# A graph attention layer on one core: the first two row groups summed in two halves of the neighbours

## The chip, the cores and the metric

The kernel runs on one core of one Trainium2 chip. The metric is device time in microseconds of one execution; lower is better. A core has TensorE (PE), VectorE (DVE), ScalarE (ACT), GpSimd (POOL), SyncE (SP) and 16 DMA engines.

## What is computed

```python
h = jnp.maximum(_layernorm(x, axis=-1), 0.0)
H = h @ W_fc + b_fc
scores = (H @ w_att[:d])[:, None] + (H @ w_att[d:])[None, :] + b_att
scores = jnp.where(adj > 0, scores, NEG_INF)
alpha = jax.nn.softmax(scores, axis=1)
out = x + alpha @ H
```

x is 4096 x 128 float32, adj is 4096 x 4096 int32 (67.1 MB). A row's own term and b_att are the same for all its neighbours and leave the softmax unchanged; neighbour j has the weight w_j = exp(H_j . w_att[d:] - bound), and a row's result is the sum of w_j * H_j over its neighbours, divided by the sum of their w_j. A row without neighbours gets the mean of H.

## The kernel before

The neighbours j are 32 tiles of 128. For each, `features[:, t]` holds w_j * (h_j @ W) and w_j, each as a part with few bits (high) and the rest (low): 258 columns. The rows i of the result are 32 tiles too, in five groups (`GROUPS`: 6, 7, 8, 7, 4 row tiles). A row tile's sum takes one PSUM bank (`BANKS`). For each group the kernel runs over all 32 tiles of neighbours: the adjacency, transposed on the host, is loaded into `ring`, VectorE turns the integers into a 0/1 `mask`, and PE multiplies the mask's 128 x 128 blocks with the features, one matmul (a "sum") of 258 columns per block, 1024 in all.

A unit (`UNITS`) is two tiles of neighbours of one group (four for the last group); two units are a pair, and a pair is one load: 72 units, 36 pairs. `ring` has 4 slots of a pair, `mask` 4 places of a unit. SP issues the load of a pair when the units that had its slot are masked (`slot_free`, line 282; load at line 304). VectorE masks a unit when it has landed and when PE has finished the unit four before it (`mask_free`, line 270; `mask_unit`, instruction at line 497). From unit 20 on ScalarE makes the last 512 columns of most masks (`share`, line 442).

Features are made from x in the first 70 us, four tiles (a chunk) at a time: VectorE's statistics (line 512) and `deviations`, ScalarE's ReLU (line 383), PE's transposes against `ident` (`turn`, line 837), ScalarE's copy (`take_turned`, line 362), PE's product with W (`features_of`, line 848), ScalarE's weighting (`weigh`, line 372), VectorE's `split` (lines 590 and 593) and ScalarE's `take_high` (line 378). Splits 0 to 2 are tiles 0 to 3, split u from 3 on is chunk u - 2, so splits 6 to 9 are tiles 16 to 31. GpSimd builds `ident` with an affine_select (line 343) and then spreads the attention vectors (`a_wide`, line 347), from which PE makes `v_rows` (line 822, copied at 393).

Each engine runs its own program in order, written out by hand: VectorE's masks, splits and other work in lines 636 to 775, PE's in lines 913 to 941. A waiting instruction holds up all behind it on its engine. When a group ends, ScalarE copies its banks to `sums` (line 455), and VectorE divides them and adds them to x (`inverse_of`, `add_sums`, `add_means`) between the masks of later groups. The row sums for the mean (line 704) stand behind masks 18 to 25. The first and last pairs of units of a group go row tile by row tile (`by_rows`, it wants both masks of the pair), so that banks come free one by one; the others go tile by tile (`by_tiles`).

## Time and profile before

| | us |
|---|---|
| median of 3 runs | 210.57 |
| lowest, highest | 207.68, 211.06 |
| the profiled execution | 207.97 |
| its span, first to last instruction | 206.2 |
| busy: PE, VectorE, ScalarE, GpSimd | 152.5, 144.5, 69.0, 1.7 |

The DMA engines moved 71.67 MB at a mean of 348 GB/s. Times in a trace count from the start of the span. A share of busy time is an average over parts with different limits, so the rows below are read by stretch.

### The profile page before, as it was taken

The numbers are of one execution on the slowest core, as the hardware profiler recorded it, in microseconds if no ns is written. First come the engines' busy times: TensorE is split into PE (matmuls) and PEld (weight loads), VectorE is DVE, ScalarE is ACT, GpSimd is POOL, SyncE is SP. The second block draws the span as 40 slices with busy tenths as digits, with TensorE's granted clock in tenths as the row PEclk, the third lists the DMA queues.
The fourth block names the chain that finished last, engine by engine and source line by source line (L and its number), as shares of the span: only waits on it lengthen the run. The fifth ranks groups of instructions, "written<-read, shape, count | busy, mean of one in ns | idle before, by whom it ended". The sixth has DMA issues, their size and how long they took to land.

```text
span 206.2 us, 3218 instructions
## 1 busy us (share of the span) xinstructions
PE 152.5 (74%) x1130; PEld 144.1 (70%) x1130; DVE 144.5 (70%) x446; ACT 69.0 (33%) x157; POOL 1.7 (1%) x10
## 2 busy tenths in 40 slices
PE   0058973946695599999767988875999997689940
PEld 0026962846694599989766988765999986688930
DVE  2415999992643969999644557788689967358992
ACT  2206655670662145432430222222522234502100
POOL 1010000000000000000000000000000000000000
PEclk9999999696999999999999999998799999999995
DMA  6999991715286699999999999999999999999821
GB/s 175 397 420 437 378 415 43 246 65 191 114 317 198 248 409 415 428 445 421 432 424 429 420 429 426 429 421 428 434 417 434 424 413 442 429 415 399 344 99 54
DMA packets 7940, 71.67 MB, mean 348 GB/s; under 512 B 881, under 2 KB 1650, under 8 KB 3314
## 3 DMA queue, kind: packets, MB, share of 16 engines
q1 hardware_dynamic: 7344, 71.18, 84.2%
q10 hardware_dynamic: 578, 0.26, 0.5%
q8 instruction: 10, 0.16, 0.3%
q14 instruction: 8, 0.07, 0.1%
HBM read 69.34 MB, written 2.10 MB: 346 GB/s over the span
## 4 chain that ended last, share of the span: by engine, by line
DMA 43%; DVE 23%; PE 16%; issue 10%; ACT 4%; POOL 0%; DVEq 0%; POOLq 0%; ACTq 0%
DMA ring<-adj 43%; PE bank L867 11%; DVE mask L497 9%; DVE features L518 2%; DVE x_sb L618 2%; ACT weighted L372 2%; PE bank L848 2%; DVE stats L512 2%; DVE weighted L704 1%; ACT relu_T L362 1%; PE bank L837 1%; DVE high_bits L590 1%; PE bank L827 1%; DVE features L593 1%; ACT relu L383 1%
## 5 line engine op out<-in xcount | busy, mean ns | idle before, releaser
L867 PE MATMUL bank<-features,mask 128*128 128x258 f32 x1024 | 135.9, 292 | 26.4 <-DVE mask L497 22.9
L867 PEld LDWEIGHTS bank<-features,mask 128*128 128x128 f32 x1024 | 129.8, 196 | 31.8 <-DVE mask L497 27.2
L497 DVE TENSOR_SCALAR mask<-ring 128x1536 fp32r<-128x1536 int32 (+3 forms) x70 | 65.9, 957 | 29.6 <-DMA ring<-adj 24.8
L442 ACT ACTIVATE mask<-ring,half_steep 128x512 fp32r<-128x512 int32 x39 | 26.1, 716 | 68.4 <-DMA ring<-adj 68.4
L618 DVE SCALAR_TENSOR_TENSOR x_sb<-sums,inv_den,x_sb 128x128 f32<-128x128 f32 x56 | 17.3, 347 | 0.6
L455 ACT COPY sums<-bank 128x258 f32<-128x258 f32 x28 | 10.5, 374 | 14.1 <-PE bank L867 12.1
L848 PE MATMUL bank<-w_sb,relu_T 128*128 128x128 f32 x64 | 10.0, 303 | 6.3 <-ACT relu_T L362 6.3
L848 PEld LDWEIGHTS bank<-w_sb,relu_T 128*128 128x128 f32 x64 | 8.7, 211 | 7.6 <-ACT relu_T L362 7.6
L372 ACT ACTIVATE weighted<-bank,w_over_std 128x128 f32<-128x128 f32 x32 | 9.2, 368 | 9.2 <-PE bank L848 7.5
L383 ACT ACTIVATE relu<-x_sb,neg_mean 128x128 f32<-128x128 f32 x32 | 9.8, 390 | 4.9 <-DVE neg_mean L527 4.9
L822 PE MATMUL bank<-w_T_and_a,a_wide 128*128 128x128 f32 x2 | 0.8, 488 | 12.9 <-POOL a_wide L347 12.9
L512 DVE BATCH_NORM_STATS2 stats<-x_sb 128x6 f32<-128x128 f32 x32 | 6.7, 279 | 4.1 <-DMA x_sb<-x 4.0
L822 PEld LDWEIGHTS bank<-w_T_and_a,a_wide 128*128 128x128 f32 x2 | 0.5, 313 | 12.8 <-issue 12.8
L590 DVE TENSOR_SCALAR high_bits<-weighted 128x512 int32<-128x512 int32 (+2 forms) x10 | 3.7, 371 | 7.8 <-ACT weighted L372 7.7
L631 DVE SCALAR_TENSOR_TENSOR x_sb<-mean_H,is_empty,x_sb 128x128 f32<-128x128 f32 x32 | 9.1, 347 | 0.0
L518 DVE SCALAR_TENSOR_TENSOR features<-relu,v_rows 128x128 fp32r<-128x128 f32 x32 | 8.6, 285 | 0.0
L704 DVE SCALAR_TENSOR_TENSOR weighted<-relu,rstd,weighted 128x128 f32<-128x128 f32 x28 | 7.9, 345 | 0.0
L362 ACT COPY relu_T<-bank 128x512 f32<-128x512 f32 x8 | 4.7, 592 | 8.3 <-PE bank L837 8.3
L378 ACT CAST features<-high_bits 128x512 fp32r<-128x512 f32 (+2 forms) x10 | 5.4, 537 | 3.3 <-DVE high_bits L590 3.2
L593 DVE TENSOR_TENSOR features<-weighted,high_bits 128x512 fp32r<-128x512 f32 (+2 forms) x10 | 5.9, 586 | 0.3
L837 PE MATMUL bank<-ident,relu 128*128 128x128 f32 x32 | 6.0, 321 | 0.1
L837 PEld LDWEIGHTS bank<-ident,relu 128*128 128x128 f32 x32 | 4.6, 168 | 1.3 <-issue 1.1
(72 smaller groups left out, 46.3 us busy)
## 6 DMA issues: line engine op xcount, KB each, us to landing
ring<-adj SPq DMA_DIRECT2D x16, 1792.0 KB, 13.4
ring<-adj SPq DMA_DIRECT2D x11, 2048.0 KB, 17.1
ring<-adj SPq DMA_DIRECT2D x7, 1536.0 KB, 8.0
ring<-adj SPq DMA_DIRECT2D x2, 768.0 KB, 6.9
x_sb<-x SPq DMA_DIRECT2D x1, 1024.0 KB, 13.6
ring<-adj SPq DMA_DIRECT2D x1, 1024.0 KB, 15.6
ring<-adj SPq DMA_DIRECT2D x4, 256.0 KB, 15.9
out<-x_sb SPq DMA_DIRECT2D x2, 448.0 KB, 10.0
```

What stands on the lines that cost most here:

```text
L372: last = nc.scalar.activation(weighted[:, u % 2, at], ps_features[:, of], ACT.Copy, scale=w_over_std[:, t:t + 1])
L383: nc.scalar.activation(relu[:, t, :], x_sb[:, t, :], ACT.Relu, bias=neg_mean[:, t:t + 1]).then_inc(relu_ready, 1)
L442: nc.scalar.activation(mask[:, n % MASKS, cols - SHARE:cols], ring[:, n // 2 % RING, end - SHARE:end], ACT.Sigmoid, bias=half_steep[:], sc ...
L455: nc.scalar.copy(sums[:, b, :], bank[:, BANKS[g][b], 0:WIDE]).then_inc(sums_copied, 1)
L497: nc.vector.tensor_scalar(mask[:, n % MASKS, 0:cols], ring[:, n // 2 % RING, begin:begin + cols], 0.0, None, ALU.is_gt).then_inc(masks_rea ...
L512: return nc.vector.bn_stats(stats[:, t, :], x_sb[:, t, :])
L518: return nc.vector.scalar_tensor_tensor(out=features[:, t, 1, 0:D], in0=relu[:, t, :], scalar=1.0, in1=v_rows[:, 1, :], op0=ALU.mult, op1= ...
L618: last = nc.vector.scalar_tensor_tensor(out=x_sb[:, row, :], in0=source, scalar=inv_den[:, row:row + 1], in1=x_sb[:, row, :], op0=ALU.mult ...
L704: last = nc.vector.scalar_tensor_tensor(out=row_sum[:, i, :], in0=relu[:, t, :], scalar=rstd[:, t:t + 1], in1=row_sum[:, i, :], op0=ALU.mu ...
L837: last = nc.tensor.transpose(ps_turned[:, q * P:(q + 1) * P], relu[:, PER * c + q, :], ident[:])
L848: last = nc.tensor.matmul(ps_features[:, q * D:(q + 1) * D], relu_T[:, c % 2, q * P:(q + 1) * P], w_sb[:], start=True, stop=True)
L867: last = nc.tensor.matmul(bank[:, BANKS[g][b], 0:WIDE], mask[:, n % MASKS, at:at + P], features[:, t, :, :].rearrange("p h d -> p (h d)"), ...
```

## The change

- The first two groups have six row tiles each and are taken in halves. `SEGMENTS` is the order of work: group 0 with neighbour tiles 0 to 15, group 1 with 0 to 15, group 0 with 16 to 31, group 1 with 16 to 31, then groups 2 and 3 (eight row tiles each) and 4 whole. Their units are 0 to 7, 8 to 15, 16 to 23, 24 to 31, 32 to 47, 48 to 63 and 64 to 71.
- ScalarE copies the banks of the first halves to `sums` (`copy_sums`), VectorE adds the banks of the second halves (`add_halves`, 12 new operations of 258 columns).
- `ident` comes by DMA: GpSimd writes a one and zeros, 129 wide; ScalarE's queue stores them in DRAM; ScalarE waits, and loads them back 128 wide.
- `ring` goes from 16384 to 12288 columns: four pairs of six row tiles, or three of eight. `mask` goes from 8192 to 10240: six places of six row tiles, or five of eight. `places_of` lays both out, and a load or mask waits for the last one that it overlaps.
- The engines' orders are new: row sums for the mean behind masks 20 to 27, groups 0 and 1 divided at units 35 to 40, the bias at 41 to 48, group 3's means behind masks 69 and 70 (before: behind the last mask). ScalarE shares the masks of segments 3 and 4 from their first unit.

```diff
-GROUPS = [(0, 6), (6, 7), (13, 8), (21, 7), (28, 4)]
-BANKS = [[0, 1, 2, 3, 4, 5], [6, 0, 1, 2, 3, 4, 5], [6, 0, 1, 2, 3, 4, 5, 7], [6, 0, 1, 2, 3, 4, 5], [4, 5, 6, 7]]
-
-ORDERS = [range(6), range(7), range(8), range(7), (3, 2, 0, 1)]
+GROUPS = [(0, 6), (6, 6), (12, 8), (20, 8), (28, 4)]
+BANKS = [[0, 1, 2, 3, 4, 5], [0, 1, 2, 3, 4, 5], [6, 7, 0, 1, 2, 3, 4, 5], [0, 1, 2, 3, 6, 7, 4, 5], [0, 1, 2, 3]]
+
+PLACES = [0, 6, 0, 8]
+
+
+SEGMENTS = [(0, 0, 16), (1, 0, 16), (0, 16, 32), (1, 16, 32), (2, 0, 32), (3, 0, 32), (4, 0, 32)]
+
+COPIED = [0, 1, 4, 5]
+ADDED = [2, 3]
 TURN_BANK, FEATURE_BANK, MEAN_BANK = 6, 7, 7
 
 RING = 4
-MASKS = 4
+RING_COLS = 24 * BLOCK
+MASK_COLS = 20 * BLOCK
...
+    for s, (g, t0, t1) in enumerate(SEGMENTS):
+        step = 4 if GROUPS[g][1] == 4 else 2
+        out += [(s, g, t, step) for t in range(t0, t1, step)]
     return out
+
+
+def places_of(widths, cols):
+
+    begins, before = [], []
+    at = 0
+    for n, width in enumerate(widths):
+        at = 0 if at + width > cols else at
+        over = [m for m in range(n) if begins[m] < at + width and at < begins[m] + widths[m]]
+        begins.append(at)
+        before.append(over[-1] if over else None)
+        at += width
+    return begins, before
...
-    SHARED = [n for n, u in enumerate(UNITS) if 20 <= n < LAST and n - FIRST[u[0]] >= 4]
+    SHARED = [n for n, u in enumerate(UNITS) if 20 <= n < LAST and (u[0] in (3, 4) or n - FIRST[u[0]] >= 4)]
...
-            before = n - MASKS
+            before = MASK_BEFORE[n]
+            if before is None:
+                return
             if closes(before):
-                engine.wait_ge(sums_done, tiles_before(UNITS[before][0] + 1))
+                engine.wait_ge(sums_done, sums_before(UNITS[before][0] + 1))
             else:
                 engine.wait_ge(units_done, sum(not closes(m) for m in range(before + 1)))
...
-                after = 2 * (pair - RING) + 2
+                after = 2 * PAIR_BEFORE[pair] + 2
...
-            nc.gpsimd.memset(ident[:], 0.0).then_inc(cleared, 1)
+            nc.gpsimd.memset(one_and_zeros[:], 0.0).then_inc(cleared, 1)
             nc.gpsimd.memset(ones_row[:], 1.0).then_inc(ones_ready, 1)
             pool.wait_ge(cleared, 1)
-            nc.gpsimd.affine_select(out=ident[:], in_=ident[:], compare_op=ALU.not_equal, fill=1.0, base=0,
-                                    pattern=[[-1, P]], channel_multiplier=1).then_inc(constants_ready, 1)
+            nc.gpsimd.memset(one_and_zeros[:, 0:1], 1.0).then_inc(one_and_zeros_ready, 1)
             nc.gpsimd.memset(half_steep[:], -0.5 * STEEP).then_inc(half_steep_ready, 1)
...
+            act.wait_ge(one_and_zeros_ready, 1)
+            act.dma_start(ident_scratch.ap().rearrange("(p d) -> p d", d=D + 1), one_and_zeros[:]).then_inc(ident_stored, 16)
+            act.wait_ge(ident_stored, 16)
+            act.dma_start(ident[:], ident_scratch.ap()[0:P * P].rearrange("(p d) -> p d", d=P)).then_inc(ident_landed, 16)
...
+            def copy_sums(s):
+                g = SEGMENTS[s][0]
+                for b in range(WIDTH[s]):
+                    act.wait_ge(sums_done, sums_before(s) + b + 1)
+                    nc.scalar.copy(sums[:, PLACES[g] + b, :], bank[:, BANKS[g][b], 0:WIDE]).then_inc(sums_copied, 1)
...
             relu_tiles(16, 32)
+            copy_sums(0)
+            row_weights_of(3)
             take_turned(4)
-            row_weights_of(3)
             act.wait_ge(w_over_std_ready, 4)
-            for u in range(6, 10):
+            weigh(6)
+            take_turned(5)
+            take_high(6)
+            copy_sums(1)
+            for u in range(7, 10):
                 weigh(u)
                 if u < 9:
                     take_turned(u - 1)
                 take_high(u)
...
+            for s in range(2, LAST_SEGMENT + 1):
                 for n in SHARED:
-                    if UNITS[n][0] == g:
+                    if UNITS[n][0] == s:
                         share(n)
-                if g < LAST_GROUP:
-                    if g > 0:
-                        act.wait_ge(sums_read, g)
-                    for b in range(width):
-                        act.wait_ge(sums_done, r0 + b + 1)
-                        nc.scalar.copy(sums[:, b, :], bank[:, BANKS[g][b], 0:WIDE]).then_inc(sums_copied, 1)
+                if s in COPIED:
+                    act.wait_ge(sums_read, 2)
+                    copy_sums(s)
...
+            def add_halves(s):
+
+                g = SEGMENTS[s][0]
+                for b in range(WIDTH[s]):
+                    dve.wait_ge(sums_done, sums_before(s) + b + 1)
+                    dve.wait_ge(sums_copied, copied_before(g) + b + 1)
+                    here = sums[:, PLACES[g] + b, :]
+                    nc.vector.tensor_tensor(here, here, bank[:, BANKS[g][b], 0:WIDE], ALU.add).then_inc(sums_added, 1)
...
             split(5)
             mask_unit(6)
+            mask_unit(7)
             deviations(2, between_2)
             for t in range(28, 32):
                 last = dot_of(t)
             scores(3, last)
-            mask_unit(7)
+            mask_unit(8)
             row_weights(3)
-            mask_unit(8)
+            for n in range(9, 12):
+                mask_unit(n)
             split(6)
-            mask_unit(9)
+            for n in range(12, 16):
+                mask_unit(n)
             split(7)
-            mask_unit(10)
+            mask_unit(16)
+            mask_unit(17)
             split(8)
-            mask_unit(11)
+            mask_unit(18)
+            mask_unit(19)
             split(9)
 
-            for n in range(12, LAST):
+            for n in range(20, LAST):
                 mask_unit(n)
...
+                if n in range(20, 28):
...
                 if n == 25:
+                    add_halves(2)
...
+                if n == 33:
+                    add_halves(3)
+                if n == 35:
+                    inverse_of(0)
+                if n in (35, 36, 37):
+                    add_sums(0, range(2 * (n - 35), 2 * (n - 34)))
+                if n == 38:
                     inverse_of(1)
-                if n in (44, 45, 46, 47):
-                    add_sums(1, range(2 * (n - 44), min(2 * (n - 43), 7)))
-                if n in (41, 42):
-                    add_means(0, range(3 * (n - 41), 3 * (n - 40)), results_ready)
-                if n in (49, 50):
-                    add_means(1, [range(0, 4), range(4, 7)][n - 49], results_ready)
-                if n == 52:
+                if n in (38, 39, 40):
+                    add_sums(1, range(2 * (n - 38), 2 * (n - 37)))
+                if n == 41:
+                    dve.wait_ge(sums_read, 2)
+                if n in range(41, 41 + CHUNKS):
+                    rows = x_sb[:, (n - 41) * PER:(n - 40) * PER, :]
+                    nc.vector.tensor_tensor(rows, rows, b_row.unsqueeze(1).to_broadcast([P, PER, D]), ALU.add).then_inc(bias_added, 1)
+                if n in (43, 44):
+                    add_means(0, range(3 * (n - 43), 3 * (n - 42)), results_ready)
+                if n in (45, 46):
+                    add_means(1, range(3 * (n - 45), 3 * (n - 44)), results_ready)
...
+                if n in (69, 70):
+                    add_means(3, range(4 * (n - 69), 4 * (n - 68)), results_ready)
...
                 if c == 0:
-                    pe.wait_ge(constants_ready, 1)
+                    pe.wait_ge(ident_landed, 16)
...
+            def bank_free(s, b):
+
+                of = BANKS[SEGMENTS[s][0]][b]
+                before = [r for r in range(s) if of in BANKS[SEGMENTS[r][0]]]
+                if before:
+                    r = before[-1]
+                    after = BANKS[SEGMENTS[r][0]].index(of) + 1
+                    if r in COPIED:
+                        pe.wait_ge(sums_copied, copied_before(r) + after)
+                    else:
+                        pe.wait_ge(sums_added, added_before(r) + after)
+                elif of == MEAN_BANK:
+                    pe.wait_ge(mean_H_ready, 1)
...
+                s = UNITS[n][0]
+                local = local_of(n)
+                if s == 0 and n > 0:
                     next_features(n // 2)
-                if (local == 0 and g > 0) or (local == COUNT[g] - 2 and g < LAST_GROUP):
+                if n == 30:
+                    pe.wait_ge(mean_wide_ready, 1)
+                    nc.tensor.matmul(ps_mean_H, mean_wide[:], w_sb[:], start=True, stop=True).then_inc(mean_H_in_psum, 1)
+                if (local == 0 and s > 0) or (local == COUNT[s] - 2 and s < LAST_SEGMENT):
                     by_rows(n)
                 else:
                     by_tiles(n)
                     if n == 0:
                         next_features(0)
                     by_tiles(n + 1)
-                if n == 26:
+                if n == 10:
+                    turn(4)
+                    features_of(4)
+                    turn(5)
+                if n == 14:
+                    features_of(5)
+                    turn(6)
+                if n == 16:
+                    features_of(6)
+                    turn(7)
+                if n == 18:
+                    features_of(7)
```

VectorE's program around splits 6 to 9, before. L497 is a mask; L590 and L593 together are one split.

```order
L497 TENSOR_SCALAR mask<-ring 128x1536
L590 TENSOR_SCALAR high_bits<-weighted 128x512
L593 TENSOR_TENSOR features<-weighted,high_bits 128x4x128
L497 TENSOR_SCALAR mask<-ring 128x1536
L590 TENSOR_SCALAR high_bits<-weighted 128x512
L593 TENSOR_TENSOR features<-weighted,high_bits 128x4x128
L497 TENSOR_SCALAR mask<-ring 128x1536
L590 TENSOR_SCALAR high_bits<-weighted 128x512
L593 TENSOR_TENSOR features<-weighted,high_bits 128x4x128
L497 TENSOR_SCALAR mask<-ring 128x1536
L590 TENSOR_SCALAR high_bits<-weighted 128x512
L593 TENSOR_TENSOR features<-weighted,high_bits 128x4x128
```

The same place after the change. L536 is a mask; L629 and L632 are a split.

```order
L536 TENSOR_SCALAR mask<-ring 128x1536 x3
L629 TENSOR_SCALAR high_bits<-weighted 128x512
L632 TENSOR_TENSOR features<-weighted,high_bits 128x4x128
L536 TENSOR_SCALAR mask<-ring 128x1536 x4
L629 TENSOR_SCALAR high_bits<-weighted 128x512
L632 TENSOR_TENSOR features<-weighted,high_bits 128x4x128
L536 TENSOR_SCALAR mask<-ring 128x1536 x2
L629 TENSOR_SCALAR high_bits<-weighted 128x512
L632 TENSOR_TENSOR features<-weighted,high_bits 128x4x128
L536 TENSOR_SCALAR mask<-ring 128x1536 x2
L629 TENSOR_SCALAR high_bits<-weighted 128x512
L632 TENSOR_TENSOR features<-weighted,high_bits 128x4x128
```

Three, four, two and two masks now stand where one each stood, in front of splits 6 to 9.

PE's program at the same place, before: L867 are sums, L837 a chunk's transposes, L848 its features.

```order
L867 MATMUL bank<-features,mask 128x258 x48
L837 MATMUL bank<-ident,relu 128x128 x4
L848 MATMUL bank<-w_sb,relu_T 128x128 x4
L837 MATMUL bank<-ident,relu 128x128 x4
L848 MATMUL bank<-w_sb,relu_T 128x128 x4
L837 MATMUL bank<-ident,relu 128x128 x4
L867 MATMUL bank<-features,mask 128x258 x24
L848 MATMUL bank<-w_sb,relu_T 128x128 x4
L837 MATMUL bank<-ident,relu 128x128 x4
L867 MATMUL bank<-features,mask 128x258 x24
L848 MATMUL bank<-w_sb,relu_T 128x128 x4
L867 MATMUL bank<-features,mask 128x258 x216
```

PE's program after: L948 are sums, L907 transposes, L918 features.

```order
L948 MATMUL bank<-features,mask 128x258 x96
L907 MATMUL bank<-ident,relu 128x128 x4
L918 MATMUL bank<-w_sb,relu_T 128x128 x4
L907 MATMUL bank<-ident,relu 128x128 x4
L948 MATMUL bank<-features,mask 128x258 x48
L918 MATMUL bank<-w_sb,relu_T 128x128 x4
L907 MATMUL bank<-ident,relu 128x128 x4
L948 MATMUL bank<-features,mask 128x258 x24
L918 MATMUL bank<-w_sb,relu_T 128x128 x4
L907 MATMUL bank<-ident,relu 128x128 x4
L948 MATMUL bank<-features,mask 128x258 x24
L918 MATMUL bank<-w_sb,relu_T 128x128 x4
```

The transposes of chunk 4 stood behind 48 sums and features 5 right behind them; now chunk 4 stands behind 96, and features 5 behind 48 more.

## Rows read from the trace of the kernel before

**Rows 1.** Windows view, eight stretches up to 100 us (its first line names columns).
```profile
core 0: us, PE busy (x) PEld busy (x) DVE busy (x) ACT busy (x) POOL busy (x), PEclk, DMA share, GB/s
0.00:20.00 20.00, 6.46 (x22) 4.67 (x22) 6.86 (x46) 5.71 (x15) 1.20 (x9) 1.00 0.92 355
20.00:30.00 10.00, 8.33 (x57) 7.89 (x56) 9.60 (x38) 5.22 (x17) 0.00 (x0) 1.00 0.99 394
30.00:40.00 10.00, 5.98 (x37) 5.10 (x36) 9.62 (x60) 5.62 (x18) 0.00 (x0) 0.86 0.40 136
40.00:50.00 10.00, 5.86 (x38) 5.65 (x37) 7.58 (x53) 5.25 (x17) 0.00 (x0) 0.84 0.35 120
50.00:60.00 10.00, 8.01 (x64) 7.53 (x63) 5.36 (x11) 5.27 (x14) 0.00 (x0) 0.96 0.53 206
60.00:70.00 10.00, 5.30 (x44) 4.90 (x43) 4.63 (x7) 4.00 (x11) 0.00 (x0) 1.00 0.76 287
70.00:80.00 10.00, 10.00 (x86) 10.00 (x85) 8.32 (x16) 3.37 (x7) 0.00 (x0) 1.00 0.89 353
80.00:100.00 20.00, 19.48 (x160) 19.09 (x159) 19.34 (x54) 7.38 (x12) 0.00 (x0) 1.00 1.01 427
```

**Rows 2.** Waits of SP's DMA queue: us in total, times, longest.
```profile
SPq L304 <- DVE mask L497: 113.1, 31, 16.0
```

**Rows 3.** Timeline of the start: start us, us, engine, line, operation.
```profile
1.75 0.36 ACTq L356 DMA_DIRECT2D w_sb<-w_fc  x1
...
2.14 1.28 ACT L383 ACT_TABLE_LOAD   x1 [2.14 <-issue]
...
12.05 0.28 POOL L343 TENSOR_SCALAR_AFFINE_SELECT ident<-ident 128x128 f32<-128x128 f32 x1 [10.99 <-issue]
...
14.10 0.37 ACT L393 COPY v_rows<-bank 128x256 f32<-128x256 f32 x1 [6.58 <-PE bank L823]
...
15.57 1.11 PE L837 MATMUL bank<-ident,relu 128*128 128x128 f32 x4
```

**Rows 4.** DMA issues on ScalarE's queue: KB each, us from issue to landing.
```profile
w_T_and_a<-w_fc_t_and_a ACTq DMA_DIRECT2D x1, 65.0 KB, 3.4
w_sb<-w_fc ACTq DMA_DIRECT2D x1, 64.0 KB, 6.9
```

**Rows 5.** Timeline, VectorE's masks and PE's idle time around 40 to 50 us.
```profile
40.54 0.95 DVE L497 TENSOR_SCALAR mask<-ring 128x1536 fp32r<-128x1536 int32 x1
...
46.73 0.95 DVE L497 TENSOR_SCALAR mask<-ring 128x1536 fp32r<-128x1536 int32 x1
...
47.73 2.95 PE L867 MATMUL bank<-features,mask 128*128 128x258 f32 x12 [4.14 <-DVE mask L497]
```

**Rows 6.** DMA issues between 35 and 52 us, loads of the ring.
```profile
ring<-adj SPq DMA_DIRECT2D x2, 1536.0 KB, 6.4
```

**Rows 7.** Timeline, the rounds of features and splits, 50 to 75 us.
```profile
50.48 0.79 PE L837 MATMUL bank<-ident,relu 128*128 128x128 f32 x4
...
51.95 1.16 PE L848 MATMUL bank<-w_sb,relu_T 128*128 128x128 f32 x8 [0.68 <-ACT relu_T L362]
...
54.37 0.43 DVE L590 TENSOR_SCALAR high_bits<-weighted 128x512 int32<-128x512 int32 x1 [0.81 <-ACT weighted L372]
...
67.33 0.43 DVE L590 TENSOR_SCALAR high_bits<-weighted 128x512 int32<-128x512 int32 x1 [3.87 <-ACT weighted L372]
...
68.40 5.56 DVE L497 TENSOR_SCALAR mask<-ring 128x1536 fp32r<-128x1536 int32 x6
69.41 5.81 PE L867 MATMUL bank<-features,mask 128*128 128x258 f32 x46 [3.29 <-DVE mask L497]
```

**Rows 8.** Groups by form, VectorE: count, busy us, mean ns.
```profile
L497 DVE TENSOR_SCALAR mask<-ring 128x1280 fp32r<-128x1280 int32 x24 | 19.6, 826 | 4.3 <-DMA ring<-adj 3.7
...
L704 DVE SCALAR_TENSOR_TENSOR weighted<-relu,rstd,weighted 128x128 f32<-128x128 f32 x28 | 7.9, 345 | 0.0
...
L709 DVE TENSOR_TENSOR weighted<-weighted 128x256 f32<-128x256 f32 x1 | 0.4, 363 | 0.0
```

211 lines of the change are left out of this document (103 added, 108 removed).

## The prediction

> **What bounds the kernel now.** I read the stretches first. The adjacency is 67.1 MB, and with x 69.2 MB have to be read. From 80 us on the DMA engines move 427 GB/s and are always busy; before that they are not: 355 GB/s to 20 us, 394 to 30, then 136, 120, 206, 287 and 353 in the five stretches of 10 us up to 80 [rows 1]. Summed up that is 7.10 + 3.94 + 1.36 + 1.20 + 2.06 + 2.87 + 3.53 = 22.06 MB by 80 us. Against 427 GB/s the 50 us from 30 to 80 lost 50 - 11.02 / 0.427 = 24.2 us. That is all this change can win in the loads, and it is also where it can lose.
>
> Second, who holds the loads back: SP's queue waited 113.1 us for VectorE's masks [rows 2]. A load waits until the units that sat in its place are masked, so the loads follow VectorE's place in its own program. VectorE in turn stands in that program behind the splits of the features, each of which waits for a round trip PE, ScalarE, VectorE.
>
> Third, the start: GpSimd's affine_select ran only at 12.05, PE's vectors came out at 14.10 and the first transposes began at 15.57 [rows 3].
>
> **The start: identity by DMA.** GpSimd no longer waits 11 us, so a_wide can be there when w_T_and_a lands, about 0.7 + 3.4 = 4.1 us [rows 4]. But ScalarE's program now stops in front of its first ReLU until the store of the pattern has landed, and the identity itself is a second transfer after it. The nearest rows for a 64 KB transfer on ScalarE's queue are 3.4 us and 6.9 us from issue to landing [rows 4]. The store is issued near 2.1 us, behind w_sb on the same queue (issued at 1.75 [rows 3], so landed at 8.7). Lower end: 2.1 + 3.4 = 5.5, then the load at 5.9 + 3.4 = 9.3. Upper end: 8.7 + 6.9 = 15.6, then 16.0 + 6.9 = 22.9. I take the store at 11 (a little behind w_sb) and the load at 11.4 + 5 = 16.4. ScalarE then loads its table (1.28 [rows 3]), makes four ReLUs and copies v_rows at 14.3, as before (14.10). The transposes start at 16.4 and not at 15.57. So I shift the start by +0.7 us, with -6 and +7 as ends. The row shows that a 64 KB transfer of 8 rows per engine took twice as long once SP's loads ran beside it. The Trainium skill (DMA: Bandwidth & Descriptors, Queues, rings and completion order) says that an engine drains a packet of some 9 to 17 descriptors from one queue before it turns to the next; by that rule our 8 per engine would go in one turn and both transfers would be near the short row. The growth from 3.4 to 6.9 speaks against it.
>
> **Up to unit 11.** VectorE's order is the old one up to mask 6, which started at 40.54 [rows 5]. Mask 7 now follows it at once, in front of the deviations: with the shift of 0.7 both are done at 42.2 and 43.1, and the load of pair 7 goes out 4.6 us earlier than before (old mask 7: 46.73 + 0.95 [rows 5]). Deviations and dots end at 48.3, mask 8 at 49.2, row weights 0.5, masks 9 to 11 at 50.7, 51.6, 52.5. Before, PE stood idle 4.14 us here, from 43.59 [rows 5]; now it has units 6 and 7 from 44.3 to 47.5 (24 sums), and ScalarE has copied the six banks before unit 8 wants them. Six mask places cover all this. Up to here the change gains.
>
> **The four rounds.** Here it gives it back. Features of tiles 16 to 31 now come out on PE behind blocks of sums, and VectorE's next masks stand behind the split that needs those features. So PE's sums and VectorE's masks take turns. Durations: 48 sums take 48 x 0.13 = 6.3 us and 24 take 3.1 (46 in 5.81 [rows 7]); transposes to split 54.37 - 50.48 = 3.9 us, of which some 0.2 was w_over_std, so 3.7; from features to split 54.37 - 51.95 = 2.4; a split 68.40 - 67.33 = 1.1; a mask 0.95, in a row 5.56 / 6 = 0.93 [rows 7].
> - Split 6: PE starts unit 8 when mask 9 is there (50.7), does units 8 to 11 (57.0), then turns tile block 4: split 6 runs 60.7 to 61.8. VectorE idles 8.2 us.
> - Split 7: masks 12 to 15 end at 65.5. PE works from 62.7 to 69.0 on units 12 to 15, features 5: split 7 runs 71.4 to 72.5. Idle 5.9.
> - Split 8: masks 16 and 17 end at 74.4, PE ends both at 77.5: split 8 runs 79.9 to 81.0. Idle 5.5.
> - Split 9: mask 18 at 81.9, 19 at 82.9, PE ends at 85.0: split 9 runs 87.4 to 88.5. Idle 4.5.
>
> VectorE idles about 24 us in these four waits. Before, the wait was 0.81 us at split 6 and 3.87 at split 9, and at 68.40 the splits were over and six masks followed at once [rows 7]. At 88.5 the changed kernel has 20 masks of six rows, 15.7 MB. The old one had 12 of them at 68.4 and then ran through ring slots that were full.
>
> **Units 20 to 27.** The row sums of the mean are still all to be made: four operations of 0.345 [rows 8], which overlap a little in line: 1.25 a unit, and a mask of 1024 columns. No row has that width; 1280 columns took 0.826 [rows 8] and 1536 took 0.95, so I go on down that line to 0.69, in a row 0.65. Eight units of 1.9 us are 15.2. add_halves(2) has no row: six additions of 258 columns, one operand in PSUM. Nearest: 0.363 for 128x256 from SBUF [rows 8]; with its gap 0.3 to 0.4 each, 2.2 us for six; the worst, if each waited for PE's bank, 3.2. Mask 27 ends at 88.5 + 15.2 + 2.2 - 1.2 = 104.7. Loads 14 and 15 fit in between. The ring now wraps differently: pair 16 has 4096 columns over pairs 12 and 13, so it waits for mask 27. By then pairs 0 to 15 are in: 2.1 + 16 x 1.573 = 27.3 MB. A load into an empty queue landed 6.4 us after its issue for 1.573 MB [rows 6], of which 3.7 are transfer: 2.7 us of start. So full flow resumes at 104.7 + 2.7 = 107.4 with 27.3 MB in.
>
> **From there to the end.** The old kernel has 22.06 + 27.4 x 0.427 = 33.8 MB in at 107.4 us [rows 1]. The lag is 6.5 MB, at 0.427 that is 15.2 us. Both then run at the rate of the DMA engines: eight-row pairs take 4.9 us, three of them in the ring leave two under way (9.8 us) while VectorE masks the third. VectorE's other work per unit (add_halves(3) 2.2, then 1.3 or less) stays under 2.47 on average, so I cost it, the moved bias and the moved add_means at nothing; the cover is the transfer, and where it fails, the excess over 9.8 - 2.7 us counts per pair. PE has 688 sums left, 688 x 0.13 = 89 us, less than 41.9 MB / 0.427 = 98 us. ScalarE has four more shares. At the very end VectorE no longer has seven mean operations after the last mask, 7 x 0.345 = 2.4 us by the row of the same kind [rows 8], but PE's last sums covered some of it: between 0 and -2.4, I take -1.
>
> **Sum.** 206.2 + 15.2 - 1 = 220.4 us of span. The profiled execution took 207.97 for 206.2 of span, so 1.8 lies around it: 222.2. The runs shown have a median of 210.57, above the profiled one; part of that may repeat, and I put the median at 223.
>
> **Rivals.**
> A, faster: the loads run through. If VectorE never waited at splits 6 to 9, because PE's sums of the second group filled the time of the features and the features were already out, unit 20 would start at 52.5 + 8 x 0.93 + 4 x 1.1 = 64.3, ahead of the loads. Full flow from pair 8 on (issued 50.7, 14.7 MB in at 53.4): 54.5 / 0.427 = 127.6, so 181 in place of 190.4 (80 + 47.1 / 0.427) for the last byte: 206.2 - 9.4 = 197 span, 199 us. It is decided by VectorE's idle time in front of the splits: it must stay under about 1 us each. For it: 24 us lost to win back, PE's idle 4.14 filled. Against it: in the program order PE makes features 4 only behind unit 11. 6%.
> B, early identity: both 64 KB transfers take the short row. Start -5 to -6, all of it handed on, since nothing else in the early chain is older: 223 - 6 = 217, down to 214 if one more round is shorter than I count. 22%; a part of it falls within 2%.
> C, late identity or slow PE: transfers at 6.9 each give +7; and PE idles 3 us and more in each round. After an idle of 4.14 us twelve sums took 2.95 us [rows 5], 0.246 each, the 1.2 GHz level; after 3.29 us they took 0.126 [rows 7], 2.4 GHz. If each round began at the low level, 12 x 0.12 = 1.4 us each, +5.6: 229 to 231. 17%.
> D, the shallower ring starves in the eight-row groups: a pair masked more than 7 us after landing leaves a gap. Half a microsecond on 20 pairs would be +10: 232. Against it: before, the masks of 1280 columns there waited 3.7 us in all for loads and hardly for anything else [rows 8]. 5%.
> The forecast itself has 50%.
>
> **How the numbers follow.** About 2% is what a measurement of this kernel tells from no change; here it means below 206.4 and above 214.8. Faster is A, 6%. Within 2% are the low part of B and errors in my chain of 8 us or more: 17%. Slower is the rest, 77%. The range goes from 212 (B with shorter rounds) to 231 (C).
>
> **What would show it.** VectorE should idle near 8, 6, 5.5 and 4.5 us in front of L629, waiting for ScalarE's weighted, and its first mask of 1024 columns should come near 88. The DMA rate should drop to nothing between the pairs from 37 to 93 us, with 27 MB in by 107, and hold 425 or more behind it. The transposes should start at 15 to 18 us. I am wrong if VectorE's waits at L629 sum to under 12 us, if unit 20 is masked before 78, or if the first transposes start before 11.

## The result and the profile after

| | before | after |
|---|---|---|
| median of 4 runs, us | 209.18 | 228.12 |
| lowest, highest | 207.68, 211.06 | 225.76, 230.24 |
| the profiled execution | 207.97 | 230.24 |
| its span | 206.2 | 228.4 |
| busy: PE, VectorE | 152.5, 144.5 | 163.4, 147.2 |

The ratio is 1.090, with an interval from 1.076 to 1.105: the change made the kernel 9% slower. (Before has one run more here than in the table ahead of the prediction.) The profile after is of the longest of its four executions, 2.1 us over the median, and the one before is near its shortest, so differences between the two profiles come out larger than those of the medians (22.2 us of span against 18.9). The forecast was 223, with a range from 212 to 231.

The windows view of the changed kernel answers to [rows 1].

```profile
core 0: us, PE busy (x) PEld busy (x) DVE busy (x) ACT busy (x) POOL busy (x), PEclk, DMA share, GB/s
0.00:20.00 20.00, 4.17 (x11) 2.46 (x12) 5.97 (x40) 3.77 (x9) 1.00 (x9) 1.00 0.93 355
20.00:30.00 10.00, 8.34 (x49) 7.79 (x49) 8.36 (x34) 6.06 (x19) 0.00 (x0) 1.00 0.80 318
30.00:40.00 10.00, 6.14 (x46) 5.20 (x44) 9.66 (x58) 5.66 (x17) 0.00 (x0) 0.96 0.47 165
40.00:50.00 10.00, 7.38 (x48) 7.00 (x48) 9.79 (x64) 7.96 (x28) 0.00 (x0) 0.87 0.81 304
50.00:60.00 10.00, 7.85 (x52) 7.72 (x52) 3.75 (x8) 0.20 (x1) 0.00 (x0) 0.83 0.68 269
60.00:70.00 10.00, 6.42 (x40) 6.11 (x40) 4.59 (x6) 2.82 (x7) 0.00 (x0) 0.83 0.40 144
70.00:80.00 10.00, 6.23 (x45) 6.03 (x45) 2.86 (x4) 4.49 (x12) 0.00 (x0) 0.84 0.64 247
80.00:90.00 10.00, 7.15 (x38) 6.91 (x38) 2.86 (x4) 2.23 (x6) 0.00 (x0) 0.67 0.39 144
90.00:100.00 10.00, 5.57 (x29) 5.41 (x28) 4.24 (x12) 4.95 (x10) 0.00 (x0) 0.67 0.35 144
100.00:110.00 10.00, 9.47 (x64) 9.29 (x64) 9.83 (x29) 4.66 (x8) 0.00 (x0) 0.80 0.82 315
110.00:120.00 10.00, 8.84 (x70) 8.29 (x69) 6.37 (x18) 1.34 (x2) 0.00 (x0) 1.00 0.77 285
120.00:140.00 20.00, 17.47 (x137) 16.47 (x137) 16.40 (x42) 5.36 (x8) 0.00 (x0) 1.00 1.00 427
```

Sum the last column as in [rows 1]: 30.45 MB are in at 120 us. The kernel before had 22.06 MB at 80 us and went on at 427 GB/s, which makes 39.1 MB at 120. The changed kernel lags by 8.7 MB, and 8.7 / 0.427 = 20.4 us of the 22.2 by which its span is longer. At 60 us the changed kernel is 2.0 MB ahead (17.66 against 15.66): up to unit 11 it gains, as forecast. It loses 10.7 MB from 60 to 120, and from 120 on the loads run at 427 GB/s again. Also look at the PEclk column: it falls to 0.83 and then to 0.67 from 80 to 100, where before stood at 1.00 from 60 to 140 us.

VectorE's timeline over the same stretch: start, duration, what ran, and in brackets the idle time in front and what ended it.

```profile
51.10 2.69 DVE L536 TENSOR_SCALAR mask<-ring 128x1536 fp32r<-128x1536 int32 x3
63.17 0.43 DVE L629 TENSOR_SCALAR high_bits<-weighted 128x512 int32<-128x512 int32 x1 [9.38 <-ACT weighted L408]
...
74.89 0.43 DVE L629 TENSOR_SCALAR high_bits<-weighted 128x512 int32<-128x512 int32 x1 [7.09 <-ACT weighted L408]
...
85.65 0.43 DVE L629 TENSOR_SCALAR high_bits<-weighted 128x512 int32<-128x512 int32 x1 [7.87 <-ACT weighted L408]
...
95.69 0.43 DVE L629 TENSOR_SCALAR high_bits<-weighted 128x512 int32<-128x512 int32 x1 [7.16 <-ACT weighted L408]
...
96.77 0.69 DVE L536 TENSOR_SCALAR mask<-ring 128x1024 fp32r<-128x1024 int32 x1
```

Its total from the waits view (us, times, longest):

```profile
DVE high_bits L629 <- ACT weighted L408: 31.5, 4, 9.4
```

These are the four waits that the prediction placed, 9.4, 7.1, 7.9 and 7.2 us long. The first mask of 1024 columns is unit 20, at 96.77.

PE's timeline there shows the other half of the turns:

```profile
52.15 7.49 PE L948 MATMUL bank<-features,mask 128*128 128x258 f32 x48 [4.38 <-DVE mask L536]
...
65.25 7.54 PE L948 MATMUL bank<-features,mask 128*128 128x258 f32 x48 [2.90 <-DVE mask L536]
...
77.88 5.50 PE L948 MATMUL bank<-features,mask 128*128 128x258 f32 x24 [3.77 <-DVE mask L536]
...
87.72 5.53 PE L948 MATMUL bank<-features,mask 128*128 128x258 f32 x24 [2.85 <-DVE mask L536]
```

While VectorE idles PE works, and before each of these blocks PE has idled 2.9 to 4.4 us for a mask. The 48 sums take 7.5 us (0.156 each) and the 24 take 5.5 (0.23 each); in [rows 7] a sum took 0.126.

The start, which answers to [rows 3], and the DMA issues that answer to [rows 4] (KB, then us from issue to landing):

```profile
10.26 0.33 ACTq L392 DMA_DIRECT2D ident<-ident_scratch  x1
...
13.10 0.35 ACT L442 COPY v_rows<-bank 128x256 f32<-128x256 f32 x1
...
17.92 1.09 PE L907 MATMUL bank<-ident,relu 128*128 128x128 f32 x4 [10.30 <-DMA ident<-ident_scratch]
```

```profile
ident_scratch<-one_and_zeros ACTq DMA_DIRECT2D x1, 64.5 KB, 8.1
w_sb<-w_fc ACTq DMA_DIRECT2D x1, 64.0 KB, 6.6
ident<-ident_scratch ACTq DMA_DIRECT2D x1, 64.0 KB, 7.5
```

The store and the load of the identity took 8.1 and 7.5 us, one behind the other. GpSimd no longer paused for 11 us, and a_wide began at 4.31 in place of 12.34. v_rows came out only a microsecond earlier than in [rows 3], behind ScalarE's first ReLUs, which had waited for the store, and the transposes began at 17.92 in place of 15.57.

### The profile page after: what moved, and what is told of

Same layout as the page of the kernel before. It is cut to its first block, busy times and chain, and to the rows that moved or that the text cites. A ratio compares the mean times of both kernels' runs of the same rounds, so it can differ in the third digit from the quotient of the medians.

```text
span 228.4 us, 3252 instructions
## 1 busy us (share of the span) xinstructions
PE 163.4 (72%) x1130; PEld 153.5 (67%) x1130; DVE 147.2 (64%) x458; ACT 70.9 (31%) x161; POOL 1.5 (1%) x10
## 4 chain that ended last, share of the span: by engine, by line
DMA 37%; DVE 33%; PE 17%; issue 6%; ACT 4%; ACTq 1%; DVEq 0%
DMA ring<-adj 30%; PE bank L948 15%; DVE mask L536 13%; DVE x_sb L673 4%; DMA ident_scratch<-one_and_zeros 4%; DVE weighted L766 3%; DMA ident<-ident_scratch 3%; DVE features L557 3%; DVE stats L551 2%; PE bank L918 2%; ACT weighted L408 2%; DVE high_bits L629 1%; DVE features L632 1%; ACT relu_T L398 1%; DVE x_sb L688 1%
## 5 line engine op out<-in xcount | busy, mean ns | idle before, releaser
L948 PE MATMUL bank<-features,mask 128*128 128x258 f32 x1024 | 145.6, 305 | 36.4 <-DVE mask L536 29.3
L948 PEld LDWEIGHTS bank<-features,mask 128*128 128x128 f32 x1024 | 138.6, 209 | 43.3 <-DVE mask L536 35.2
L536 DVE TENSOR_SCALAR mask<-ring 128x1536 fp32r<-128x1536 int32 (+2 forms) x70 | 64.6, 942 | 23.8 <-DMA ring<-adj 20.7
L430 ACT ACTIVATE mask<-ring,half_steep 128x512 fp32r<-128x512 int32 x43 | 28.7, 716 | 72.2 <-DMA ring<-adj 65.8
L629 DVE TENSOR_SCALAR high_bits<-weighted 128x512 int32<-128x512 int32 (+2 forms) x10 | 3.7, 370 | 31.5 <-ACT weighted L408 31.5
L437 ACT COPY sums<-bank 128x258 f32<-128x258 f32 x28 | 9.9, 373 | 14.1 <-PE bank L948 12.6
L918 PE MATMUL bank<-w_sb,relu_T 128*128 128x128 f32 x64 | 10.5, 316 | 5.0 <-ACT relu_T L398 5.0
L918 PEld LDWEIGHTS bank<-w_sb,relu_T 128*128 128x128 f32 x64 | 9.5, 226 | 6.1 <-ACT relu_T L398 6.1
L907 PE MATMUL bank<-ident,relu 128*128 128x128 f32 x32 | 5.8, 312 | 10.4 <-DMA ident<-ident_scratch 10.3
L907 PEld LDWEIGHTS bank<-ident,relu 128*128 128x128 f32 x32 | 4.4, 162 | 11.7 <-issue 11.4
L632 DVE TENSOR_TENSOR features<-weighted,high_bits 128x512 fp32r<-128x512 f32 (+2 forms) x10 | 5.9, 586 | 0.3
L796 DVE TENSOR_TENSOR x_sb<-x_sb,lines 128x512 f32<-128x512 f32 x8 | 5.5, 685 | 0.0
```

What stands on the lines that cost most here:

```text
L430: nc.scalar.activation(mask[:, MASK_AT[n] + cols - SHARE:MASK_AT[n] + cols], ring[:, begin + cols - SHARE:begin + cols], ACT.Sigmoid, bias ...
L536: nc.vector.tensor_scalar(mask[:, MASK_AT[n]:MASK_AT[n] + cols], ring[:, begin:begin + cols], 0.0, None, ALU.is_gt).then_inc(masks_ready, 1)
L907: last = nc.tensor.transpose(ps_turned[:, q * P:(q + 1) * P], relu[:, PER * c + q, :], ident[:])
L918: last = nc.tensor.matmul(ps_features[:, q * D:(q + 1) * D], relu_T[:, c % 2, q * P:(q + 1) * P], w_sb[:], start=True, stop=True)
L948: last = nc.tensor.matmul(bank[:, BANKS[g][b], 0:WIDE], mask[:, at:at + P], features[:, t, :, :].rearrange("p h d -> p (h d)"), start=(t = ...
```

## The experiments

Ratios are to the kernel before, which ran beside them on the same chip. There were four such groups, and its medians in them were 209.56 (the kernels with early features alone, with PE kept busy, and the first two on the identity), 210.84 (the next two on the identity, and the larger ring with late and with early features), 208.65 (masks in front; all three edits) and 211.25 (the end). Unless said otherwise a kernel's numbers are the median of four runs, and all kernels compute the whole result.

**The first question: is it the place of the features in PE's order?** One kernel brings the features of tiles 16 to 31 forward on PE, and with them two steps on ScalarE. VectorE's order stays as the change wrote it.

```diff
-                if n == 10:
+                if n == 6:
                     turn(4)
                     features_of(4)
                     turn(5)
-                if n == 14:
+                if n == 8:
                     features_of(5)
                     turn(6)
-                if n == 16:
+                if n == 10:
                     features_of(6)
                     turn(7)
-                if n == 18:
+                if n == 12:
                     features_of(7)
...
             copy_sums(0)
+            take_turned(4)
             row_weights_of(3)
-            take_turned(4)
...
-            copy_sums(1)
             for u in range(7, 10):
                 weigh(u)
                 if u < 9:
                     take_turned(u - 1)
+                else:
+                    copy_sums(1)
                 take_high(u)
```

> The changed kernel with only the place of the late features moved: PE turns chunk 4 and makes its features right behind unit 7, features 5 behind unit 9, 6 behind unit 11, 7 behind unit 13; ScalarE copies the banks of the second segment only behind its last weighting. Theory (PE's sums and VectorE's masks take turns because the features stand behind 96 and 48 sums): VectorE's idle time in front of the four late splits falls from 31.5 us to under 10, its first mask of 1024 columns comes near 70 us and not at 96.8, 27.3 MB are in by about 88 us, and the span is about 202 us, 26 less than the changed kernel and 4 less than before. Rival 1 (taking the neighbours in halves, with more adding and a smaller ring, is what costs): over 220 us. Rival 2 (the DMA engines are late because the ring is smaller): the split waits go, and the loads still stop for over 20 us in sum between 40 and 110 us; 215 or more.

Measured: 200.64 us, ratio 0.959 (0.952 to 0.966), span 199.2. VectorE's timeline, last split and unit 20:

```profile
65.62 0.43 DVE L630 TENSOR_SCALAR high_bits<-weighted 128x512 int32<-128x512 int32 x1 [0.58 <-ACT weighted L408]
...
67.42 0.69 DVE L537 TENSOR_SCALAR mask<-ring 128x1024 fp32r<-128x1024 int32 x1 [0.64 <-PE bank L949]
```

The four waits fell from 31.5 us to 1.0, unit 20 came at 67.42 in place of 96.77, and the windows show the loads resumed:

```profile
50.00:60.00 10.00, 9.02 (x78) 8.81 (x77) 9.90 (x17) 4.54 (x13) 0.00 (x0) 1.00 0.70 271
60.00:70.00 10.00, 10.00 (x86) 10.00 (x86) 7.60 (x16) 7.54 (x19) 0.00 (x0) 1.00 1.00 428
```

So with this order the two halves, the narrower groups, the rings, the 12 additions and the identity together gain 8.9 us (200.64 against 209.56). What made the kernel slower by 19 is the place of the late features in PE's program, with the two steps of ScalarE that go with it; the run does not separate these. The same steps placed a few units earlier are worth 27 us. Part of that is PE's clock, whose mean from 50 to 100 us rose from 0.77 to 1.00; a kernel below prices it. It is also the condition of rival A (VectorE's idle time under 1 us at each split), with a time near the one given for it.

**The opposite repair: VectorE's masks in front of the splits.** PE's order stays, and VectorE makes all masks that PE needs before each split waits.

```diff
-            for n in range(9, 12):
+            for n in range(9, 16):
                 mask_unit(n)
             split(6)
-            for n in range(12, 16):
-                mask_unit(n)
-            split(7)
             mask_unit(16)
             mask_unit(17)
-            split(8)
+            split(7)
             mask_unit(18)
             mask_unit(19)
+            split(8)
             split(9)
```

> The changed kernel with PE's program as it is (features late) and only VectorE's masks moved in front of the splits: masks 9 to 15, split 6, masks 16 and 17, split 7, masks 18 and 19, splits 8 and 9. It tells whether the loss lies in PE's place of the features alone or in the two orders together. Theory (they lose because they take turns: VectorE idles while PE sums, then PE idles while VectorE masks): the splits still wait, but PE no longer stands idle 3 to 4 us in front of units 12, 16 and 18 and keeps its higher clock; the first mask of 1024 columns comes near 83 in place of 96.8 us and the time is 212 to 217. Rival (the late features alone set the rounds): the first mask of 1024 columns above 92 us and the time above 222.

Measured: 213.73 us, ratio 1.022 (1.014 to 1.031), span 211.1. Unit 20 at 79.48, somewhat earlier than expected. From its waits view:

```profile
PE bank L946 <- DVE mask L536: 20.2, 19, 4.4
...
DVE high_bits L629 <- ACT weighted L408: 13.0, 4, 4.5
```

The waits at the splits fell to 13.0 and PE's waits for masks from 29.3 to 20.2. This gives back 14 of the 19 us with PE's program untouched; some of it is again the clock, 0.90 from 50 to 100 us in place of 0.77. The loss belongs to the pair of orders, each waiting for the other. Breaking it from either side works, and from PE's side better: there the waits at the splits fell to 1.0 us, here to 13.0.

**The clock.** PE's sums in the rounds took longer than predicted. To separate the clock from the turns, this kernel keeps the changed one's order and lets PE multiply the identity with W (42 products that nobody reads) while it would wait for a mask.

```diff
+            def keep_busy(n):
+                count, weighed = {8: (14, 6), 12: (7, 7), 16: (9, 8), 18: (6, 9), 20: (6, 10)}.get(n, (0, 0))
+                if count:
+                    pe.wait_ge(weighted_ready, weighed)
+                for _ in range(count):
+                    nc.tensor.matmul(ps_features[:, 0:D], ident[:], w_sb[:], start=True, stop=True)
...
+                keep_busy(n)
                 if (local == 0 and s > 0) or (local == COUNT[s] - 2 and s < LAST_SEGMENT):
```

> The changed kernel with PE kept busy in the gaps of the four rounds: 14, 7, 9, 6 and 6 extra products of the identity with W, whose results nobody uses, in front of units 8, 12, 16, 18 and 20. Theory on the size of the loss (24 sums took 5.5 us in rounds 3 and 4 because PE had stood idle 3 to 4 us and was granted its lower clock): the granted clock between 50 and 100 us rises from 0.67 to 0.87 to 0.95 or more, 24 sums take 3.2 us, VectorE's waits fall from 31.5 to about 25 us and the span by 5 to 7 us. Rival (the clock falls for another reason than idle time): the sums stay at 0.2 us each and the extra products only cost, 0 to +3 us.

Measured: 221.54 us (221.25 to 221.69), ratio 1.059 (1.051 to 1.066), span 219.7. PE's timeline:

```profile
51.78 5.97 PE L948 MATMUL bank<-features,mask 128*128 128x258 f32 x48 [1.24 <-DVE mask L536]
...
63.36 6.04 PE L948 MATMUL bank<-features,mask 128*128 128x258 f32 x48 [0.23 <-DVE mask L536]
...
74.49 3.15 PE L948 MATMUL bank<-features,mask 128*128 128x258 f32 x24 [0.70 <-DVE mask L536]
...
81.82 3.15 PE L948 MATMUL bank<-features,mask 128*128 128x258 f32 x24 [0.45 <-DVE mask L536]
```

The sums take 0.124 to 0.131 us again, the granted clock from 50 to 100 us is 0.99 in place of 0.77, and VectorE's waits at the splits are 7.9, 5.6, 5.4 and 4.4 us, 23.2 in all. Unit 20 comes at 88.14. The prediction had 8.2, 5.9, 5.5 and 4.5, and 88.5. So by the medians 6.6 us of the loss are the clock, and the rest of the chain was priced within 1 us. How much the clock takes differs from execution to execution: the four of the changed kernel had mean granted clocks of 0.915, 0.921, 0.942 and 0.948 and took 230.24, 228.94, 225.76 and 227.29 us, those of this kernel 0.964 to 0.974. The profile above shows the lowest of them.

**The identity.** Two kernels isolate it: the changed kernel with affine_select again, and the kernel before with the identity by DMA.

```diff
-            nc.gpsimd.memset(one_and_zeros[:], 0.0).then_inc(cleared, 1)
+            nc.gpsimd.memset(ident[:], 0.0).then_inc(cleared, 1)
...
-            nc.gpsimd.memset(one_and_zeros[:, 0:1], 1.0).then_inc(one_and_zeros_ready, 1)
+            nc.gpsimd.affine_select(out=ident[:], in_=ident[:], compare_op=ALU.not_equal, fill=1.0, base=0,
+                                    pattern=[[-1, P]], channel_multiplier=1).then_inc(constants_ready, 1)
...
-            act.wait_ge(one_and_zeros_ready, 1)
-            act.dma_start(ident_scratch.ap().rearrange("(p d) -> p d", d=D + 1), one_and_zeros[:]).then_inc(ident_stored, 16)
-            act.wait_ge(ident_stored, 16)
-            act.dma_start(ident[:], ident_scratch.ap()[0:P * P].rearrange("(p d) -> p d", d=P)).then_inc(ident_landed, 16)
```

> The changed kernel with one part undone: the identity comes from GpSimd's affine_select again, ScalarE waits for nothing at the start. My theory (the identity's round trip costs a little and the rounds cost the rest): the first transposes start near 15.6 us and not at 17.9, everything behind moves forward by about 2.3 us, VectorE still idles 29 to 33 us in front of the four late splits, and the kernel stays about 17 us slower than before (near 226). Rival (the start is what lost the time): the time falls by 8 us or more, and the waits at the splits shrink with it.

Measured: 225.97 us, ratio 1.072 (1.060 to 1.083), span 224.9; transposes at 16.06, unit 20 at 93.62. That is 2.2 us less than the changed kernel by the medians, close to the 1.9 us by which the transposes came earlier. Unit 20 came 3.2 us earlier: besides the start, the four blocks of sums took 1.2 us less in this profile (8.71, 6.04, 4.58 and 5.53 us). The interval overlaps that of the change, so the size is not settled by this run alone.

The reverse edit on the kernel before:

> The kernel before with the identity by DMA alone (stored, waited for on ScalarE and loaded back). Theory: the transposes start near 17.9 in place of 15.57 us, and what follows in the first 70 us moves by the same 2.3 us, since it is one chain; span 208 to 209, +1% over before. Rival (the early chain has slack behind it, in loads still under way): no change of the span beyond 0.5 us. Second rival (removing GpSimd's wait of 11 us gains): faster by 2 us or more.

Measured, in ten runs: 211.61 us, ratio 1.006 (1.000 to 1.012), span 210.8; transposes at 17.51 in place of 15.57. The sign is that of the kernel above, and the span is above what was expected. A part of the reason is in its windows: from 50 to 60 us the granted clock was 0.50, where [rows 1] has 0.96. In both kernels twelve sums took 2.95 us behind an idle time of PE (4.14 us before, 4.48 here). Before, the chunk's products with W behind them took 1.16 us; here they took 2.08 us, and so did the next chunk's. Why the level came back late was not tried, nor whether this makes up the whole of the difference.

The identity's price on top of the early features, in place of on top of the slow order (the edits of the first and this experiment together):

> The kernel with the features early (e2_early) and in addition the identity by affine_select again. Theory (the start's delay by the two transfers is passed on where the early chain bounds): transposes near 15.7 in place of 17.8 us and the time 1.5 to 2.3 us below e2_early, about 198.5. Rival (with the rounds gone the loads have slack and the start is hidden): the same as e2_early within 0.5 us.

Measured: 198.87 us (198.51 to 199.21), ratio 0.949 (0.938 to 0.961), span 197.1, transposes at 15.76. Against the early features alone it is 1.8 us less: the identity costs about 2 us in both orders.

The DMA itself can be made cheaper. Here, on top of the early features, the store is the second instruction on ScalarE's queue and w_sb goes last.

```diff
-            act.dma_start(line[:], b_a_b_att.unsqueeze(0)).then_inc(line_landed, 16)
-            act.dma_start(w_sb[:], w_fc).then_inc(w_landed, 16)
-
             act.wait_ge(one_and_zeros_ready, 1)
             act.dma_start(ident_scratch.ap().rearrange("(p d) -> p d", d=D + 1), one_and_zeros[:]).then_inc(ident_stored, 16)
+            act.dma_start(line[:], b_a_b_att.unsqueeze(0)).then_inc(line_landed, 16)
             act.wait_ge(ident_stored, 16)
             act.dma_start(ident[:], ident_scratch.ap()[0:P * P].rearrange("(p d) -> p d", d=P)).then_inc(ident_landed, 16)
+            act.dma_start(w_sb[:], w_fc).then_inc(w_landed, 16)
```

> The kernel with the features early (e2_early) and in addition the identity's store as the second transfer on ScalarE's queue, the load back in front of w_sb. Theory (each of the two transfers took 7 to 8 us because it stood behind others on its queue and beside SP's loads): the store lands near 6 us, the identity near 12, w_sb near 15; the transposes start at 12 to 13 in place of 17.8 us and the time falls by 3 to 5 us, to about 197. Rival (a 64 KB transfer takes 7 us beside SP's loads wherever it stands): transposes at 16 us or later, no more than 2 us gained.

Measured: 198.51 us (198.23 to 198.77), ratio 0.948 (0.937 to 0.959), span 196.4, transposes at 14.26. Its DMA issues:

```profile
ident_scratch<-one_and_zeros ACTq DMA_DIRECT2D x1, 64.5 KB, 4.4
ident<-ident_scratch ACTq DMA_DIRECT2D x1, 64.0 KB, 8.5
w_sb<-w_fc ACTq DMA_DIRECT2D x1, 64.0 KB, 10.8
```

The store took 4.4 us in place of 8.1, but the load still took 8.5. The start of the transposes lies between the two expectations. The time is level with affine_select (198.51 against 198.87): the identity by DMA is then no loss, and hardly a gain.

**The rings.** The changed kernel with 32 blocks of ring and 16 of masks, the sizes of before (`RING` only counts the semaphores for pairs under way):

```diff
-RING = 4
+RING = 6
-RING_COLS = 24 * BLOCK
-MASK_COLS = 20 * BLOCK
+RING_COLS = 32 * BLOCK
+MASK_COLS = 16 * BLOCK
```

> The changed kernel with the ring and the masks at their old sizes (16384 and 8192 columns: five pairs of six row tiles or four of eight; five masks or four), with the features still late. Theory (the rounds lose the time, and the ring only sets how much is loaded ahead when they end): VectorE's waits in front of the splits stay at 31 to 33 us; one pair more is in when they end, pair 16 waits for mask 25 instead of 27, and the span falls by 3 to 6 us. Rival (three slots of eight row tiles starve the loads in the later groups): the loads, at 427 GB/s from 120 us on now, get faster there, and the span falls by 8 us or more. Six masks are worth nothing by the theory: no wait of a mask for PE beyond 3 us in all.

Measured: 224.89 us, ratio 1.072 (1.053 to 1.091), span 222.9. Its windows:

```profile
20.00:30.00 10.00, 8.22 (x51) 7.66 (x51) 8.69 (x36) 5.74 (x18) 0.00 (x0) 1.00 1.01 426
30.00:40.00 10.00, 6.33 (x45) 5.46 (x44) 9.66 (x59) 5.73 (x18) 0.00 (x0) 0.93 0.57 223
```

Against 318 and 165 GB/s the larger ring took more in before VectorE fell behind, and the kernel is 3.2 us shorter by the medians (the intervals overlap). The two profiles differ by 5.5 us of span, and this is not all the ring. PE's timeline has the same idle times in front of the four blocks, and 7.50, 7.58 and 5.50 us for the first three, but then:

```profile
87.30 3.13 PE L948 MATMUL bank<-features,mask 128*128 128x258 f32 x24 [2.85 <-DVE mask L536]
```

The changed kernel's profile has 5.53 us for these 24 sums, behind the same 2.85 us of idle time. Unit 20 then came at 93.61, 3.2 us earlier. The four places for masks cost something: ScalarE's masks waited 17.5 us for PE in place of 6.3 (VectorE's 2.3), where no more than 3 us in all was expected, and the loads ran at 388 and 375 GB/s from 120 to 140 us, where the changed kernel had 427. Behind 140 us both load at the full rate: three pairs of eight are enough, and rival D is out.

With the early features:

> The kernel with the features early (e2_early) and in addition ring and masks at their old sizes. Theory (what is left of the loads' standstill is from 25 to 57 us, where the ring is full while the first splits run): one pair more is loaded ahead, 1.57 MB or 3.7 us of transfer; the time falls by 2 to 4 us, to about 197.5. Rival A (VectorE bounds it now): no change within 1 us. Rival B (five and four masks are too few): VectorE waits for PE over 4 us in all and the time rises.

Measured, in five runs: 200.16 us (198.69 to 200.44), ratio 0.956 (0.945 to 0.967), span 196.9. The gain over the smaller ring is 0.5 us and not the 3 of before. From its waits view:

```profile
ACT mask L430 <- PE bank L949: 17.4, 8, 3.8
...
DVE mask L537 <- PE bank L949: 6.6, 4, 2.3
```

The loads were again ahead early (422 and 240 GB/s from 20 to 40 us, against 324 and 163), but fell to 385 GB/s from 70 to 80 and 354 from 100 to 110, where the early features alone kept 428 and 433. Both makers of masks now wait for PE with fewer places to write to; with the early features alone VectorE's masks waited 0.6 us for it and ScalarE's not at all. That the waits ate the gain is the likely reading; no run with both large sizes was made, and so it is argued, not shown.

All three edits, early features, affine_select and the larger ring:

> The kernel with the features early, the identity by affine_select and the ring and masks at their old sizes: is there a version below the two singles (198.87 and 200.16)? If the loads are the bound, what each lets in earlier adds up: 197 to 198. If VectorE and PE bound it between 50 and 120 us, it is the same as with affine_select alone, 198.5 to 199.5.

Measured: 198.46 us (198.04 to 199.14), ratio 0.950 (0.942 to 0.958), span 196.3. It is level with the kernel without the ring edit (198.87). The larger ring showed a gain only where VectorE is late, and there the intervals overlap.

**The end.** The change puts group 3's mean operations in front of the last masks. Here they stand behind them again, on top of the early features and the faster identity. The kernel with that edit and the same one without it ran side by side.

```diff
-                if n in (69, 70):
-                    add_means(3, range(4 * (n - 69), 4 * (n - 68)), results_ready)
...
+            add_means(3, range(8), results_ready)
             inverse_of(LAST_GROUP)
```

> The kernel with features early and the identity's transfers in front (e8_early_fast), and in addition group 3's means behind the last mask again, as in the kernel before. In the last 20 us VectorE runs without a gap from 176 to 186.5 us, and eight mean operations stand in front of mask 70 and of the last masks (1.05 us each four), while PE idles 1.05 us in front of its last 32 sums and VectorE 1.81 us behind the last masks. Theory (the change put this work on the path at the end): PE's last sums start about 1 us earlier, and the time falls by 1 us against the same kernel with the means in front. Rival (the end is set by the last load): no change.

> The same kernel as e8_early_fast once more, beside e11_means_last on the same chip, so that a difference of 1 us can be told: 198.2 to 198.8 as before.

Measured: 197.18 us (197.02 to 198.04), ratio 0.943 (0.932 to 0.954), span 195.4, with the means last, and 198.69 us (198.20 to 199.31), ratio 0.950 (0.939 to 0.962), span 196.4, with them in front. The timeline's last part with the means in front:

```profile
182.16 1.14 DVE L688 SCALAR_TENSOR_TENSOR x_sb<-mean_H,is_empty,x_sb 128x128 f32<-128x128 f32 x4
...
184.22 4.11 PE L948 MATMUL bank<-features,mask 128*128 128x258 f32 x32 [1.04 <-DVE mask L536]
185.14 1.42 DVE L840 TENSOR_SCALAR mask<-ring 128x512 fp32r<-128x512 int32 x4
```

And PE's last block with the means behind:

```profile
176.85 10.48 PE L947 MATMUL bank<-features,mask 128*128 128x258 f32 x80 [0.83 <-DVE mask L536]
```

With the means in front mask 70 is 1.0 us later (183.22 against 182.22) and the last four are 2.1 us later (185.14 against 183.09), and PE idles 1.04 us before its last 32 sums; with the means behind, it does its last 80 without a gap. All four runs of the one lie under all four of the other. This is the fastest version found, 5.7% under the kernel before.

## Why the prediction was right

The verdict and the mechanism were right. The measured 228.1 lies inside the range, 5.1 us over the forecast of 223 and 0.9 under the 229 of rival C: what ran was the forecast's chain and, on top, the clock half of rival C, which the sum had put at nothing. Three terms were off, the sums in the rounds, the start and the end. That the miss is no larger owes something to the last step of the sum: the profile's 230.2 is 8.0 over the 222.2 added up, 2.1 of that is the profile's distance from the median, and 0.8 had been added to reach 223.

- **The turns of PE and VectorE: right, and shown from both sides.** Waits of 8.2, 5.9, 5.5 and 4.5 us were placed in front of L629, and 9.4, 7.1, 7.9 and 7.2 stand there. Taking the turns apart on PE's side won 27 us, on VectorE's side 14. None of the three signs that would have made the prediction wrong came in: the waits summed to 31.5 and not under 12, unit 20 came at 96.8 and not before 78, the transposes at 17.9 and not before 11. The loads did stop between the pairs: in steps of 2 us the rate was 0 at 36, 64, 76, 84, 86, 96 and 110 us.
- **The 0.13 us for a sum in the rounds: mis-sized.** The blocks were priced at 6.3, 6.3, 3.1 and 3.1 us and took 7.5, 7.5, 5.5 and 5.5: 7.3 us more, nearly all of the 7.4 us by which the waits were longer. With the start's 1.3, and 0.4 less for masks and splits, they make up the 8.3 us by which unit 20 was late. With PE kept busy the sums and the waits fell to the predicted values and 6.6 us went. This is the clock half of rival C, which was priced at 5.6. The rows at hand pointed both ways (the low level behind 4.14 us of idle time, the high one behind 3.29), and the forecast's own rounds gave PE idle times of 3 us and more, so half of C's price would have been a fairer term than nothing. The 7.3 us are those of this one execution: in the profile with the larger ring and the same orders the blocks took 4.9 us more than priced.
- **Start +0.7 us: low by 1.3 to 1.5.** (16.4 against 15.57 is 0.8; the sum took 0.7.) Mask 11 ended at 53.8 and not at 52.5, the transposes began at 17.92 and not at 16.4. The store (8.1) and the load (7.5) both were near the long row of [rows 4] where I had taken 5 us for the load. The store landed near 10.3, close to the 11 taken. Returning to affine_select gave 2 us back. Rival B wanted two short transfers: even with the store second on its queue only one of the two was short. The row's growth from 3.4 to 6.9 was what held here: the three 64 KB transfers beside SP's loads took 6.6 to 8.1 us. What the prediction drew from the rule of the Trainium skill (DMA: Bandwidth & Descriptors, Queues, rings and completion order), that both would be near the short row, did not come in; whether an engine takes turns as the page says no run here shows.
- **Units 20 to 27: right in size.** 14.9 us in place of 16.2. A mask of 1024 columns took 0.69 as taken from the line of [rows 8], and an addition of halves 0.418, six of them in line 2.1 us, for 2.2.
- **The lag: 20.4 us for 15.2.** Mask 27 ended at 111.6, 6.9 us late (unit 20's 8.3 less what units 20 to 27 gave back), and finer windows show that the loads stood still until it was made, as forecast:

```profile
108.00:112.00 4.00, 4.00 (x35) 4.00 (x35) 3.97 (x12) 1.66 (x4) 0.00 (x0) 1.00 0.16 68
112.00:116.00 4.00, 3.54 (x29) 3.34 (x28) 3.23 (x9) 0.32 (x1) 0.00 (x0) 1.00 0.88 274
```

From 100 us on that is 286, 433 and 68 GB/s in steps of four, so 27.6 MB are in at 112 us; from there to 120 another 2.85 came, as much as 6.7 us at the full rate. Full flow in effect from 113.3, with 27.6 MB, stands for the forecast's 107.4 with 27.3. That is 5.9 us later with 0.3 MB (0.7 us) more: the 5.2 us that are missing.
- **The full rate behind it: right.** 427 GB/s from 120 us on, with three slots of eight. Rival D did not occur, and a larger ring loaded no faster there.
- **The end, -1 us: wrong sign.** The span grew 1.8 us beyond the lag. The rows that would have said so stand in the trace of before, VectorE's last part:

```profile
194.53 1.43 DVE L770 TENSOR_SCALAR mask<-ring 128x512 fp32r<-128x512 int32 x4
195.88 1.92 DVE L631 SCALAR_TENSOR_TENSOR x_sb<-mean_H,is_empty,x_sb 128x128 f32<-128x128 f32 x7
198.17 0.17 DVE L606 TENSOR_REDUCE den<-bank 128x4 f32<-128x8 f32 x1 [0.37 <-PE bank L867]
```

Before, the seven means behind the last masks ended 0.37 us before PE's last sums: they were free. Where the change puts them, they delay the last masks, for which PE waits:

```profile
216.08 1.14 DVE L688 SCALAR_TENSOR_TENSOR x_sb<-mean_H,is_empty,x_sb 128x128 f32<-128x128 f32 x4
217.13 1.43 DVE L840 TENSOR_SCALAR mask<-ring 128x512 fp32r<-128x512 int32 x4
```

VectorE works there without a gap until 218.6. The pair of kernels on this edit shows 1.0 us of span and 1.5 us by the medians for it, on top of the early features. The forecast's -1 and the measured 1.8 are 2.8 us apart; what makes up the rest is open.

With the lag's 5.2 us and the end's 2.8 the 220.4 of the forecast become the 228.4 of the profile. What stays open: the halves were never measured without the new order and group sizes, and the kernel before was never tried with its late features earlier, so how much of the 8.9 us that the repaired kernel wins is the halves' is not known.

## What to carry to other kernels

Where engines run their programs in order, find for each block of work who makes its input and issue that maker *in front of* the blocks that would hold it up, on every engine that it passes; if A's block stands in front of what B waits for and B's next block stands behind that wait, they take turns, and the time is the sum of both. A restructuring that is good in itself (here the change with its order repaired gained 9 us) can be hidden by one such place (27 us, the clock's part included), so read the waits before dropping it. Work put in front of the last producer is not free because it was visible at the end: look whether the last consumer covered it already.

## What the runs showed of the hardware

- The granted clock fell in rounds with idle times of only 2.85 to 4.38 us in front of blocks of 24 to 48 sums: 0.67 on average from 80 to 100 us, and 24 sums at 0.23 us each. In the kernel before, sums behind 3.29 us of idle time ran at 0.126 [rows 7]. And the same 24 sums behind the same 2.85 us of idle time took 5.53 us in the changed kernel's profile and 3.13 in that of the larger ring. So the idle time right in front of a block did not tell which of the two levels it got; why these differ was not settled. Forty-two products that nobody read turned a clock of 0.77 into 0.99 and won 6.6 us.
- The runs of one kernel spread less where PE was kept fed: by 0.4 to 1.1 us over four runs (221.25 to 221.69 with the unused products, 200.58 to 200.98 with early features; by 1.8 over five with the larger ring too). The runs of the kernel before spread by 3.4 us and those of the changed one by 4.5.
- A transfer of 64 or 65 KB took 3.3 to 3.9 us as the first on ScalarE's queue, 4.4 or 4.5 as the second, issued at 1.19 us, and 6.0 to 10.8 when it was issued behind SP's first loads of the adjacency (1.65 us), over all profiles. Whether its place on the queue or the loads beside it made it slow was not separated.
- GpSimd stood still for 11.0 to 11.5 us in front of affine_select in the four kernels that had it there. In those that had only memsets it waited 3.0 to 3.5 us for w_T_and_a and no longer: a_wide began at 4.31 us in place of 12.34.
